# Moving the value transposes of the attention stage into the block of transposes behind Q's projection

## The chip, the core and the metric

The kernel runs on one core of one Trainium2 chip. The metric is the device time of one execution in microseconds (us). The engines are TensorE (PE: matmuls, and PEld for its weight loads), VectorE (DVE), ScalarE (ACT), GpSimd (POOL) and SyncE (SP), which here only issues DMAs. Each engine runs its own instruction stream in order, and the streams meet at semaphores that are written out by hand.

## The reference, cut to what matters

```python
x = x + attn(cond(x, cond_128, ...), w_attn, w_proj, adapter_wte, gating)
x = x + ffn(cond2(x, ...), ...)

def attn(x, w_attn, w_proj, adapter_wte, gating):      # 32 sequences of 64 tokens, 1024 channels, 32 heads of 32
    q, k, v = split(einsum('btc,oc->bto', x, w_attn), 3)
    q, k = rope(q), rope(k)
    y = softmax(causal(q @ k.T / sqrt(32))) @ v         # per head
    y = y + gating * softmax(q @ ak.T / sqrt(1024)) @ av  # 10 adapter rows, ak and av from the same w_attn
    return einsum('btc,oc->bto', y, w_proj)
```

The change touches only the attention, ahead of `w_proj`. What comes before it (mixing of `x`) and behind it (output projection, convolution, routed low-rank feed-forward) is as it was.

## The kernel before, in words

The attention stage is a loop over 8 groups `g` of 4 heads (128 channels) and, within each, over 4 units `u` of 512 tokens: 32 units, `n = 4 g + u`. In unit `n` TensorE projects K, Q and V of the unit, 24 matmuls of 128x512 each (three for each of 8 channel chunks, `project_qkv`; operands are split into a high and a low part, `w_hi` and `w_lo` for the weights), into the PSUM banks `bK`, `bQ` and `bV`. The attention proper lags by one unit: in unit `n` it is done for unit `n - 1`. TensorE's order in a unit is:

1. `attend_scores(n-1)`, 32 small matmuls (64 in the trace, which shows the two passes of a float32 matmul apart), line 903;
2. `turn_values(n-1)`, four 128x128 transposes of `vT` into `bV`, line 969;
3. the projections of K and Q, line 957; in the first unit of a group also `project_adapter`, line 981;
4. `attend_transposes(n-1)`, four transposes of the adapter weights (line 912) and eight of the softmax's result `prob` (line 919);
5. the projection of V, line 957;
6. `attend_values(n-1)`, two matmuls for the adapter (line 931, which read `aT`) and 32 small ones (line 940, which read `pT` and the values `vs`), into `bY` and, since no bank is free, into `bK`.

So the next K projection also waits until ScalarE has copied the half of `y` that lies in `bK`.

ScalarE copies V's projection out of PSUM (`vT`, line 1291), copies the turned values into `vs` (four copies, line 1304), takes the exponentials (lines 1187 and 1189), copies the transposed weights (`aT`, line 1194, `pT`, line 1197), and copies `y` (`ysb`, line 1203). VectorE masks and normalises the scores and rotates K and Q.

In the last unit of a group (`refill`, units 3, 7, ... 27: seven of them) the weights of the next group are brought in: SP issues one DMA of 1536 KB into `w_st` (line 759), and ScalarE rounds K's, Q's and V's third to `w_hi` (`split_hi`, line 1182), each in its place in the stream of its unit: K's ahead of `attend_copies`, Q's behind it, V's behind `vT`. VectorE then forms `w_lo` (`split_lo`, line 1371). SP issues that DMA behind the store of the last prepared weights (`store_prep`), which it issues behind the store of `y`. After the loop, the last unit's attention is interleaved with the output projection (line 1036).

Of the kernel before, what the change touches and what calls it, by code (L numbers as in the profile page):

```python
# [28 lines left out]
ACT = mybir.ActivationFunctionType  # L29
# [3 lines left out]
P = 128  # L33
NB, NC, L = 32, 64, 1024
# [3 lines left out]
NG = L // P  # L38
UT = 512
NU = TOK // UT  # L40
# [3 lines left out]
NP = NB // 2  # L44
# [23 lines left out]
Q_, K_, V_ = 0, 1, 2  # L68
# [5 lines left out]
def wait(eng, sem, value):  # L74

    if not isinstance(value, int) or value > 0:
        eng.wait_ge(sem, value)
# [304 lines left out]
def program(nc, d, psum, z, zbase, y_dram, x1_dram, w_forms, ctx_dram, aggb_dram, weights, out):  # L382
# [8 lines left out]
    with ExitStack() as ctx:  # L391
        def sem(name):
            return ctx.enter_context(nc.semaphore(name))
# [37 lines left out]
        ident = both.take("ident", [P, P])  # L431
# [17 lines left out]
        vT = sb("vT", [P, UT])  # L449
        vs = sb("vs", [P, UP // 2, 2, GH * HD])  # L450
# [41 lines left out]
        bS, bY, bQ, bK, bV = bank[0:4], bank[4], bank[5], bank[6], bank[7]  # L492
# [16 lines left out]
        v_tr = sem("a_v_tr")  # L509
        vs_set = sem("a_vs_set")  # L510
# [28 lines left out]
        y_mm = sem("a_y_mm")  # L539
        y_copied = sem("a_y_copied")  # L540
# [50 lines left out]
        def place(t):  # L591

            return t.manual_sbuf_range[0]

        parts, ctx_out, z_mm, z_sum, z_lo = mixing(
            nc, ctx, d, psum, z, z[:, :, :, :, :].bitcast(F32),
            [Space(nc, "f", zbase + u * Z + Z // 2).take(f"z_raw{u}", [P, KC, UT]) for u in range(NU)], ctx_dram, aggb_dram,
            (wst, whi, wlo, whi_f, w_first, w_hi, w_lo),
            (place(kbd_pad), place(qr), place(bbase), [place(t) for t in (x8[0], prob[0], pT[0], vs)],
             [place(t) for t in (vT, aprob, aT, ysb)], attn.at))  # L600
# [4 lines left out]
        def first(g, u):  # L605
            return isinstance(g, int) and g == 0 and u == 0

        def last(g):
            return isinstance(g, int) and g == NG - 1

        def refill(g, u):

            return u == NU - 1 and not last(g)

        def y_banks(m):

            return (bY, bK) if m < NG * NU - 1 else (bS[3], bS[0])

        def y_done(m):

            return 2 * (m + 1)

        def prep_at(n):

            g, u = n // NU, n % NU
            return 2 * g + u - 1 if u in (1, 2) else None
# [261 lines left out]
        def _(pe):  # L888
# [20 lines left out]
            def attend_transposes(m):  # L909
                pe.wait_ge(aprobs, 2 * m + 2)  # L910
                for i in range(UP):
                    tr = pe.transpose(bAT[:, i * P:(i + 1) * P], aprob[:, i, :].bitcast(F32),  # L912
                                      ident[:])
                tr.then_inc(a_tr, 1)
                wait(pe, pT_copied, 2 * m)
                for t, dst in enumerate(bPT):
                    pe.wait_ge(probs, 2 * m + t + 1)
                    for j in range(4):
                        tr = pe.transpose(dst[:, j * P:(j + 1) * P],  # L919
                                          prob[t][:, 2 * j:2 * j + 2, :].rearrange("p h k -> p (h k)"), ident[:])  # L920
                    tr.then_inc(p_tr, 1)
# [40 lines left out]
            def project_qkv(x, dst, g, u):  # L962
                for c in range(KC):
                    project_chunk(x, dst, g, u, c)

            def turn_values(m):
                pe.wait_ge(vT_copied, m + 1)
                for i in range(UP):
                    tr = pe.transpose(bV[:, i * P:(i + 1) * P], vT[:, i * P:(i + 1) * P], ident[:])  # L969
                tr.then_inc(v_tr, 1)  # L970

            def project_adapter(g, n):
# [13 lines left out]
            def unit_step(g, u):  # L986
                n = NU * g + u
                groups = g + 1 if u else g
                att = not first(g, u)
                if g == 0:  # L990
                    pe.wait_ge(z_lo, UP * (u + 1))
                if att:
                    attend_scores(n - 1, groups)
                    turn_values(n - 1)
                wait(pe, turned[K_], n)
                wait(pe, y_copied, y_done(n - 2) - 1)
                project_qkv(K_, bK, g, u)
                wait(pe, turned[Q_], n)
                project_qkv(Q_, bQ, g, u)
                if u == 0:  # L1000
                    project_adapter(g, n)
                if att:
                    attend_transposes(n - 1)
                wait(pe, vs_set, n)
                project_qkv(V_, bV, g, u)
                if att:
                    attend_values(n - 1, groups)
# [103 lines left out]
            m = NG * NU - 1  # L1111
# [53 lines left out]
        def _(act):  # L1165
# [10 lines left out]
            def split_hi(x, g, n):  # L1176

                act.wait_ge(w_in, 16 * g)
                wait(act, mm_done[x], n)
                if x != Q_:  # L1180
                    wait(act, akv_mm, g)
                act.activation(whi[:, :, x, :], wst[:, :, x, :], ACT.Copy).then_inc(w_hi[x], 1)
# [8 lines left out]
            def attend_copies(m):  # L1191
                act.wait_ge(a_tr, m + 1)
                wait(act, y_mm, m)
                act.activation(aT[:], bAT[:], ACT.Copy).then_inc(aT_copied, 1)  # L1194
                for t, src in enumerate(bPT):
                    act.wait_ge(p_tr, 2 * m + t + 1)
                    act.activation(pT[t][:].rearrange("p s q -> p (s q)"), src[:], ACT.Copy).then_inc(pT_copied, 1)

            def y_copy(m):
                act.wait_ge(y_mm, m + 1)  # L1200
                wait(act, y_out, 16 * m)
                for r in (1, 0):
                    act.activation(ysb[:].rearrange("p (s r t) -> p r s t", r=2, t=P)[:, r],
                                   y_banks(m)[r][:, 0:UP * NC].rearrange("p (s t) -> p s t", t=P), ACT.Copy).then_inc(y_copied, 1)
# [52 lines left out]
            def unit_step(g, u):  # L1257
                n = NU * g + u
                att = not first(g, u)
                if att:  # L1260
                    attend_exp(n - 1)
                if refill(g, u):
                    split_hi(K_, g + 1, n + 1)
                if n == 0:
                    for i in range(NP - 5, NP - 2):
                        mix_scalar.high(act, i)
                if u == 0:
                    act.wait_ge(akv_mm, g + 1)
                    wait(act, ak_tr, g)
                    act.activation(akv[:], bAD[:, 0:2 * P], ACT.Copy).then_inc(akv_copied, 1)  # L1270
                if n == 0:
                    mix_scalar.high(act, NP - 2)
                if att:
                    attend_copies(n - 1)
                if refill(g, u):
                    split_hi(Q_, g + 1, n + 1)
                if u == 0:
                    act.wait_ge(ak_tr, g + 1)
                    wait(act, scores, 2 * n)
                    act.activation(kbd[:, :, NC:KW], bAD[:, AKT:AKT + NA].rearrange("p (b a) -> p b a", b=1)  # L1280
                                   .broadcast_to([P, UB, NA]), ACT.Copy).then_inc(akbd_set, 1)
                if n == 0:
                    mix_scalar.high(act, NP - 1)
                if prep_at(n) is not None:
                    prep_high(prep_at(n))
                if n == NG * NU - 1:
                    for f in form_order(0)[:4]:
                        high(0, f)
                act.wait_ge(mm_done[V_], n + 1)
                wait(act, v_tr, n)  # L1290
                act.activation(vT[:], bV[:], ACT.Copy).then_inc(vT_copied, 1)
                if refill(g, u):
                    split_hi(V_, g + 1, n + 1)
                if n == NG * NU - 1:
                    high(0, S2)
                if att:
                    y_copy(n - 1)
                act.wait_ge(v_tr, n + 1)
                wait(act, y_mm, n)
                if n == 0:  # L1300
                    act.wait_ge(z_mm, NP)
                for b in range(2):
                    for r in range(2):
                        cp = act.activation(vs[NC * r:NC * (r + 1), :, b, :],  # L1304
                                            bV[NC * b:NC * (b + 1), :].rearrange("p (s r c) -> p r s c", r=2, c=P)[:, r],
                                            ACT.Copy)
                cp.then_inc(vs_set, 1)

            for n in range(NG * NU):
                unit_step(n // NU, n % NU)  # L1310
            m = NG * NU - 1
# [550 lines left out]
```

## Time and profile before

| | |
|---|---|
| median of 3 runs | 1137.48 us (1137.21 to 1139.59) |
| the profiled execution: time, span | 1138.46 us, 1136.7 us |
| PE busy | 1126.2 us, 99% of the span |
| DVE busy | 922.0 us, 81% |
| ACT busy | 361.1 us, 32% |
| chain that ended last | PE 86%, DMA 6%, DVE 3%, issue 3%, ACT 1%, SPq 1% |
| ACT L1304, `a_vs` | 128 copies, 48.5 us, 379 ns each |
| ACT L1182, `w_hi`, idle before it | 70.8 us, 7 times, until the DMA of `w_st` |

The span runs from the first to the last instruction; the time of an execution holds some 1.8 us around it. Matmuls overlap in the records, so the length of a block of them is read from start to start and not from the busy column. The mean granted clock of TensorE is 1.000 of full speed over the span.

### The profile page before, as it was taken

What the parts mean: (1) busy time and instruction counts of PE and PEld (TensorE: products, weight loads), DVE (VectorE), ACT (ScalarE), POOL (GpSimd) and SP (SyncE); (2) the same over time, 40 slices, a digit from 0 to 9 for tenths busy, and PEclk for the clock granted to TensorE, in tenths of its full rate; (3) what the DMA queues carried; (4) which work ended last, traced back from release to release, by engine and by line L of the source; (5) the groups of instructions that cost most, each with busy time, mean ns of one, the idle gap of its engine ahead of it and who ended that gap; (6) DMA issues with size and microseconds to landing.
All of it is one profiled execution on the core that took longest, in us unless ns stands there. A gap on an engine that the chain in (4) does not pass through costs nothing.

```text
span 1136.7 us, 23651 instructions
## 1 busy us (share of the span) xinstructions
PE 1126.2 (99%) x9688; PEld 947.3 (83%) x9688; DVE 922.0 (81%) x1740; ACT 361.1 (32%) x697; POOL 53.7 (5%) x23
## 2 busy tenths in 40 slices
PE   9999999999999999999999999999999999999998
PEld 6888788888888788888888888878888888888887
DVE  5999879879889789799798799888767777887674
ACT  5433333333342342433434334323222221222210
POOL 0000000000000000000000000110000022221112
PEclk9999999999999999999999999999999999999999
DMA  6515215114124025034133177884549933333312
GB/s 220 185 57 162 72 29 168 66 56 149 58 77 151 35 84 168 12 111 140 33 100 131 55 275 264 325 248 156 185 130 354 340 92 99 98 116 117 98 37 93
DMA packets 99708, 151.94 MB, mean 134 GB/s; under 512 B 7442, under 2 KB 84114, under 8 KB 96914
## 3 DMA queue, kind: packets, MB, share of 16 engines
q1 hardware_dynamic: 98594, 135.76, 36.8%
q10 hardware_dynamic: 1008, 14.68, 3.1%
q8 instruction: 77, 1.26, 0.5%
q14 instruction: 29, 0.24, 0.1%
HBM read 95.88 MB, written 54.54 MB: 132 GB/s over the span
## 4 chain that ended last, share of the span: by engine, by line
PE 86%; DMA 6%; DVE 3%; issue 3%; ACT 1%; SPq 1%; POOLq 0%; POOL 0%; DVEq 0%; ACTq 0%
PE psum L957 40%; PE psum L1036 23%; PE psum L1054 5%; PE psum L903 2%; PE psum L940 2%; PE psum L919 2%; PE psum L276 2%; DMA w_forms<-a_prep_hi_two 2%; DMA w_st<-in_wqkvT 2%; PE psum L1088 2%; DMA y_scratch<-a_ysb 2%; PE psum L1070 2%; PE psum L969 1%; PE psum L912 1%; PE psum L981 1%
## 5 line engine op out<-in xcount | busy, mean ns | idle before, releaser
L957 PE MATMUL psum<-z,w_hi 128*128 128x512 f32 x1536 | 481.9, 395 | 0.8 <-issue 0.6
L957 PEld LDWEIGHTS psum<-z,w_hi 128*128 128x128 f32 x1536 | 282.5, 188 | 57.9 <-issue 2.0
L957 PE MATMUL psum<-z,w_lo 128*128 128x512 f32 x768 | 300.3, 391 | 0.0
L1036 PE MATMUL psum<-f_wform,f_act_hi 128*128 128x512 f32 (+1 forms) x912 | 279.9, 389 | 2.0 <-DVE f_u L1506 1.4
L1036 PEld LDWEIGHTS psum<-f_wform,f_act_hi 128*128 128x128 f32 x912 | 167.9, 188 | 36.4 <-issue 2.8
L1036 PE MATMUL psum<-f_wform,f_act_lo 128*128 128x512 f32 (+1 forms) x456 | 176.1, 386 | 0.0
L957 PEld LDWEIGHTS psum<-z,w_lo 128*128 128x128 f32 x768 | 144.1, 188 | 31.5
L1036 PEld LDWEIGHTS psum<-f_wform,f_act_lo 128*128 128x128 f32 x456 | 85.7, 188 | 17.6
L878 POOL TENSOR_TENSOR f_xn<-f_x,_bbase 128x1024 f32<-128x1024 f32 x16 | 51.2, 3197 | 1033.2 <-DVE f_x L1532 701.6
L1231 ACT ACTIVATE f_act_hi<-f_act_sum 128x512 fp32r<-128x512 f32 x64 | 40.3, 632 | 119.5 <-DVE f_act_sum L1481 47.9
L1231 ACT ACTIVATE f_act_hi<-f_raw 128x512 fp32r<-128x512 f32 x56 | 33.7, 626 | 102.2 <-DVE f_raw L1564 64.5
L1406 DVE TENSOR_TENSOR a_prob<-psum,a_mask 128x512 f32<-128x512 f32 x64 | 44.0, 687 | 24.6 <-PE psum L903 24.6
L1487 DVE TENSOR_TENSOR f_act_lo<-f_act_sum,f_act_hi 128x512 fp32r<-128x512 f32 x64 | 49.0, 769 | 16.8 <-ACT f_act_hi L1231 16.8
L1487 DVE TENSOR_TENSOR f_act_lo<-f_raw,f_act_hi 128x512 fp32r<-128x512 f32 x56 | 37.2, 689 | 28.0 <-ACT f_act_hi L1231 27.9
L1194 ACT ACTIVATE a_aT<-psum 128x512 fp32r<-128x512 f32 x32 | 19.1, 598 | 122.0 <-PE psum L912 121.9
L1187 ACT ACTIVATE a_prob<-a_prob 128x512 f32<-128x512 f32 x64 | 40.5, 633 | 53.9 <-DVE a_prob L1411 53.3
L1304 ACT ACTIVATE a_vs<-psum 64x256 f32<-64x256 f32 x128 | 48.5, 379 | 25.2 <-PE psum L969 24.1
L1384 DVE STREAM_SHUFFLE a_rot<-psum 128x512 f32<-128x512 f32 x64 | 47.1, 736 | 0.0
L1411 DVE TENSOR_TENSOR a_prob<-a_prob,a_stat 128x512 f32<-128x512 f32 x64 | 44.3, 692 | 2.2
L1387 DVE TENSOR_TENSOR a_rot<-a_rot,a_sin 128x512 f32<-128x512 f32 x64 | 44.3, 692 | 2.2
L1423 DVE TENSOR_TENSOR a_prob<-a_prob,a_stat 128x512 f32<-128x512 f32 x64 | 44.3, 692 | 2.2
L1409 DVE TENSOR_REDUCE a_stat<-a_prob 128x8 f32<-128x512 f32 x64 | 43.9, 686 | 2.2
(172 smaller groups left out, 1478.2 us busy)
## 6 DMA issues: line engine op xcount, KB each, us to landing
w_forms<-f_prep_lo SPq DMA_DIRECT2D x16, 896.0 KB, 5.2
f_wform<-w_forms SPq DMA_DIRECT2D x7, 2048.0 KB, 13.6
f_wform<-w_forms ACTq DMA_DIRECT2D x7, 2048.0 KB, 17.6
w_st<-in_wqkvT SPq DMA_DIRECT2D x7, 1536.0 KB, 6.6
w_forms<-f_prep_hi SPq DMA_DIRECT2D x16, 640.0 KB, 6.2
m_x<-in_x SPq DMA_DIRECT2D x16, 512.0 KB, 5.4
y_scratch<-a_ysb SPq DMA_DIRECT2D x32, 256.0 KB, 2.8
f_raw<-y_scratch SPq DMA_DIRECT2D x8, 1024.0 KB, 5.8
```

The lines of the kernel that those rows point to most:

```text
L878: pool.tensor_tensor(xn[:, t, :].rearrange("p (m q) -> p q m", q=PH), x1[:, t, :].rearrange("p (q m) -> p q m", q=PH), bbase[:].rearrange( ...
L957: mm = pe.matmul(dst, w[:, c, x, :], zs, start=(c == 0 and i == 0), stop=(c == KC - 1 and i == 2))
L1036: mm = pe.matmul((prod_bank[i], bank[0])[part][:, cols], a[:, c, :], wform[i][:, w, c, cols], start=(i < 4 and c == 0 and n == 0), stop=(c ...
L1054: mm = pe.matmul(conv_banks(p)[:, o:o + P], x8[p % 2][:, CONV * b + g, j:j + P], toep[:, g, j, :], start=(j == 0), stop=(j == 1))
L1231: act.activation(act_hi[f][:], src, ACT.Copy).then_inc(act_hi_set, 1)
L1304: cp = act.activation(vs[NC * r:NC * (r + 1), :, b, :], bV[NC * b:NC * (b + 1), :].rearrange("p (s r c) -> p r s c", r=2, c=P)[:, r], ACT. ...
L1384: dve.stream_shuffle(rot[:], src[:], HALF_SWAP).then_inc(turned[x], 1)
L1387: dve.tensor_tensor(r, r, tab[1], ALU.mult).then_inc(rot_step, 1)
L1406: dve.tensor_tensor(prob[t][:].rearrange("p (h s) k -> p h s k", h=2), score_slots[:, 2 * t:2 * t + 2, :, 0:NC], maskb, ALU.add).then_inc( ...
L1411: dve.tensor_tensor(prob[t][:], prob[t][:], spread(t, 0), ALU.subtract).then_inc(shifted, 1)
L1423: dve.tensor_tensor(prob[t][:], prob[t][:], spread(t, 2), ALU.mult).then_inc(probs, 1)
L1487: dve.tensor_tensor(act_lo[f][:], src, act_hi[f][:].bitcast(F32), ALU.subtract).then_inc(act_set, 1)
```

## The change

`turn_values(n-1)` is moved from behind the scores to the head of the block of transposes behind Q's projection. Its result goes to the bank `bY` (`v_bank`), which is free there once `y` of unit `n - 2` is copied; only the last unit's transposes stay behind their scores and on `bV`. V's projection no longer waits for `vs`. On ScalarE the four copies into `vs` become `spread_values`, and stand ahead of `attend_copies` of the next unit, where they were behind `y_copy`. In the refill units `y_copy` now stands ahead of V's `split_hi`.

```diff
+        def v_bank(m):
+            return bY if m < NG * NU - 1 else bV
...
             def turn_values(m):
                 pe.wait_ge(vT_copied, m + 1)
+                if m < NG * NU - 1:
+                    wait(pe, y_copied, y_done(m - 1))
                 for i in range(UP):
-                    tr = pe.transpose(bV[:, i * P:(i + 1) * P], vT[:, i * P:(i + 1) * P], ident[:])
+                    tr = pe.transpose(v_bank(m)[:, i * P:(i + 1) * P], vT[:, i * P:(i + 1) * P], ident[:])
                 tr.then_inc(v_tr, 1)
...
                 if att:
                     attend_scores(n - 1, groups)
-                    turn_values(n - 1)
                 wait(pe, turned[K_], n)
...
                 if att:
+                    turn_values(n - 1)
                     attend_transposes(n - 1)
-                wait(pe, vs_set, n)
                 project_qkv(V_, bV, g, u)
...
+            def spread_values(m):
+                act.wait_ge(v_tr, m + 1)
+                wait(act, y_mm, m)
+                if m == 0:
+                    act.wait_ge(z_mm, NP)
+                for b in range(2):
+                    for r in range(2):
+                        cp = act.activation(vs[NC * r:NC * (r + 1), :, b, :],
+                                            v_bank(m)[NC * b:NC * (b + 1), :].rearrange("p (s r c) -> p r s c", r=2, c=P)[:, r],
+                                            ACT.Copy)
+                cp.then_inc(vs_set, 1)
...
                 if att:
+                    spread_values(n - 1)
                     attend_copies(n - 1)
...
                 act.activation(vT[:], bV[:], ACT.Copy).then_inc(vT_copied, 1)
-                if refill(g, u):
-                    split_hi(V_, g + 1, n + 1)
                 if n == NG * NU - 1:
                     high(0, S2)
                 if att:
                     y_copy(n - 1)
-                act.wait_ge(v_tr, n + 1)
-                wait(act, y_mm, n)
-                if n == 0:
-                    act.wait_ge(z_mm, NP)
-                for b in range(2):
...
+                if refill(g, u):
+                    split_hi(V_, g + 1, n + 1)
+                if n == NG * NU - 1:
+                    spread_values(n)
```

TensorE at the border of two units (units 1 and 2). Before, the last small matmuls of `attend_values`, the scores, V's transposes (`a_vT`), then K's projection:

```order
L940 MATMUL psum<-a_pT_111,a_vs 32x64 x2
L903 MATMUL psum<-a_kbd,a_qr 64x74 x32
L969 MATMUL psum<-_ident,a_vT 128x128 x4
L957 MATMUL psum<-z,w_hi 128x512 x2
L957 MATMUL psum<-z,w_lo 128x512
```

Of the change, at the same place (line numbers are those of the changed file):

```order
L944 MATMUL psum<-a_pT_111,a_vs 32x64 x2
L907 MATMUL psum<-a_kbd,a_qr 64x74 x32
L961 MATMUL psum<-z,w_hi 128x512 x2
L961 MATMUL psum<-z,w_lo 128x512
L961 MATMUL psum<-z,w_hi 128x512 x2
```

The projection now follows the scores with nothing between them.

TensorE behind Q's projection in unit 2. Before:

```order
L957 MATMUL psum<-z,w_lo 128x512
L912 MATMUL psum<-_ident,a_aprob 128x128 x4
L919 MATMUL psum<-_ident,a_prob_108 128x128 x4
L919 MATMUL psum<-_ident,a_prob_109 128x128 x4
L957 MATMUL psum<-z,w_hi 128x512 x2
L957 MATMUL psum<-z,w_lo 128x512
```

Of the change:

```order
L961 MATMUL psum<-z,w_lo 128x512
L975 MATMUL psum<-_ident,a_vT 128x128 x4
L916 MATMUL psum<-_ident,a_aprob 128x128 x4
L923 MATMUL psum<-_ident,a_prob_108 128x128 x4
L923 MATMUL psum<-_ident,a_prob_109 128x128 x4
L961 MATMUL psum<-z,w_hi 128x512 x2
L961 MATMUL psum<-z,w_lo 128x512
```

The block has grown from twelve transposes to sixteen.

ScalarE in the first refill unit, unit 3. Before, from the exponentials of unit 2 to the copies of the turned values of unit 3:

```order
L1187 ACTIVATE a_prob_109<-a_prob_109 128x512
L1189 ACTIVATE a_atmp<-a_atmp 128x160
L1182 ACTIVATE w_hi<-w_st 128x8x128
L1194 ACTIVATE a_aT<-psum 128x512
L1197 ACTIVATE a_pT_110<-psum 128x512
L1197 ACTIVATE a_pT_111<-psum 128x512
L1182 ACTIVATE w_hi<-w_st 128x8x128
L1291 ACTIVATE a_vT<-psum 128x512
L1182 ACTIVATE w_hi<-w_st 128x8x128
L1203 ACTIVATE a_ysb<-psum 128x2x128 x2
L1304 ACTIVATE a_vs<-psum 64x2x128 x4
```

Of the change:

```order
L1192 ACTIVATE a_prob_109<-a_prob_109 128x512
L1194 ACTIVATE a_atmp<-a_atmp 128x160
L1187 ACTIVATE w_hi<-w_st 128x8x128
L1211 ACTIVATE a_vs<-psum 64x2x128 x4
L1199 ACTIVATE a_aT<-psum 128x512
L1202 ACTIVATE a_pT_110<-psum 128x512
L1202 ACTIVATE a_pT_111<-psum 128x512
L1187 ACTIVATE w_hi<-w_st 128x8x128
L1309 ACTIVATE a_vT<-psum 128x512
L1220 ACTIVATE a_ysb<-psum 128x2x128 x2
L1187 ACTIVATE w_hi<-w_st 128x8x128
```

The four copies into `a_vs` (of unit 2) now stand between K's rounding and the copies of `aT` and `pT`, and the copies of `y` (`a_ysb`) have changed places with the last `w_hi`, V's.

## Rows read from the trace of the kernel before

**Rows 1.** The page, busy time of each engine.
```profile
PE 1126.2 (99%) x9688; PEld 947.3 (83%) x9688; DVE 922.0 (81%) x1740; ACT 361.1 (32%) x697; POOL 53.7 (5%) x23
```

**Rows 2.** Waits of PE: who for whom, us in total, times, longest.
```profile
PE psum L940 <- ACT a_pT L1197: 0.8, 3, 0.4
...
PE psum L969 <- ACT a_vT L1291: 0.4, 1, 0.4
```

**Rows 3.** Timeline of PE in an ordinary unit: start us, us, instruction.
```profile
160.85 0.60 PE L912 MATMUL psum<-_ident,a_aprob 128*128 128x128 f32 x4
161.28 1.04 PE L919 MATMUL psum<-_ident,a_prob 128*128 128x128 f32 x8
...
169.71 0.65 PE L969 MATMUL psum<-_ident,a_vT 128*128 128x128 f32 x4
170.12 0.72 PE L957 MATMUL psum<-z,w_hi 128*128 128x512 f32 x2
170.68 0.40 PE L957 MATMUL psum<-z,w_lo 128*128 128x512 f32 x1
170.91 0.40 PE L957 MATMUL psum<-z,w_hi 128*128 128x512 f32 x1
```

**Rows 4.** Timeline of PE where a wide product follows line 940 directly.
```profile
726.28 0.74 PE L1036 MATMUL psum<-f_wform,f_act_hi 128*128 128x512 f32 x2
726.87 0.40 PE L1036 MATMUL psum<-f_wform,f_act_lo 128*128 128x512 f32 x1
```

**Rows 5.** Timeline of ACT, the copies into `vs` in an ordinary unit.
```profile
170.40 1.55 ACT L1304 ACTIVATE a_vs<-psum 64x256 f32<-64x256 f32 x4 [0.88 <-PE psum L969]
```

**Rows 6.** Timeline of ACT in the first refill unit.
```profile
122.50 1.06 ACT L1182 ACTIVATE w_hi<-w_st 128x1024 fp32r<-128x1024 f32 x1 [11.03 <-DMA w_st<-in_wqkvT]
123.58 0.60 ACT L1194 ACTIVATE a_aT<-psum 128x512 fp32r<-128x512 f32 x1
124.08 1.08 ACT L1197 ACTIVATE a_pT<-psum 128x512 f32<-128x512 f32 x2
...
125.98 0.61 ACT L1291 ACTIVATE a_vT<-psum 128x512 f32<-128x512 f32 x1
126.45 1.08 ACT L1182 ACTIVATE w_hi<-w_st 128x1024 fp32r<-128x1024 f32 x1
127.40 0.68 ACT L1203 ACTIVATE a_ysb<-psum 128x256 f32<-128x256 f32 x2
```

**Rows 7.** Timeline of PE at the same place.
```profile
125.30 0.85 PE L940 MATMUL psum<-a_pT,a_vs 64*32 64x64 f32 x64 [0.44 <-ACT a_pT L1197]
126.17 0.93 PE L903 MATMUL psum<-a_kbd,a_qr 32*64 32x74 f32 x64
127.03 0.66 PE L969 MATMUL psum<-_ident,a_vT 128*128 128x128 f32 x4
127.91 0.70 PE L957 MATMUL psum<-z,w_hi 128*128 128x512 f32 x2 [0.22 <-issue]
```

**Rows 8.** Timelines of ACT and PE in the refill units of groups 1, 4 and 6.
```profile
205.16 1.06 ACT L1182 ACTIVATE w_hi<-w_st 128x1024 fp32r<-128x1024 f32 x1 [9.92 <-DMA w_st<-in_wqkvT]
...
210.73 0.49 PE L957 MATMUL psum<-z,w_hi 128*128 128x512 f32 x1
...
454.55 1.06 ACT L1182 ACTIVATE w_hi<-w_st 128x1024 fp32r<-128x1024 f32 x1 [9.27 <-DMA w_st<-in_wqkvT]
...
460.77 0.72 PE L957 MATMUL psum<-z,w_hi 128*128 128x512 f32 x2
...
620.64 1.06 ACT L1182 ACTIVATE w_hi<-w_st 128x1024 fp32r<-128x1024 f32 x1 [9.49 <-DMA w_st<-in_wqkvT]
...
627.09 0.70 PE L957 MATMUL psum<-z,w_hi 128*128 128x512 f32 x2 [0.21 <-issue]
```

**Rows 9.** Timelines of DVE and PE in unit 4: end of the softmax, first transposes.
```profile
138.30 0.23 DVE L1440 CAST a_aprob<-a_aprob 128x160 fp32r<-128x160 f32 x1
...
139.98 0.66 PE L912 MATMUL psum<-_ident,a_aprob 128*128 128x128 f32 x4
```

More of the change, by code:

```diff
@@ L1297, in unit_step @@
                     y_copy(n - 1)
-                act.wait_ge(v_tr, n + 1)
-                wait(act, y_mm, n)
-                if n == 0:
-                    act.wait_ge(z_mm, NP)
-                for b in range(2):
[L1303 to L1307, printed above, removed]
+                if refill(g, u):
+                    split_hi(V_, g + 1, n + 1)
+                if n == NG * NU - 1:
+                    spread_values(n)
             for n in range(NG * NU):
```

## The prediction

> **What bounds the kernel now.** I read the page first: TensorE is busy for 1126.2 of the 1136.7 us of the span [rows 1], so a change pays only where TensorE starts something sooner, or costs where it starts something later. Then the waits of TensorE: in the attention stage hardly any are left. The largest that belongs to the part changed is that of the small matmuls of `attend_values` for `pT`, 0.8 us over three places, and one wait of 0.4 us of the first value transposes for `vT` [rows 2]. So the change can't win much by taking waits away. What it can do is to alter the length of TensorE's own blocks, and to bring back waits where ScalarE is nearly late. Where that is, the timeline of ScalarE shows: in a refill unit it stands still for 11.03 us until the weights of the next group have landed, and all it has to do in that unit comes after, in a row [rows 6], while TensorE is some 2 us from needing it [rows 7]. I call the start of K's rounding L below (122.50 in the first such unit), and L is when the DMA has landed.
>
> **The 24 ordinary borders of units.** Removed: the four value transposes behind the scores, 169.71 to 170.12, so 0.41 us. Added: four in the block behind Q's projection. The four adapter transposes there last from 160.85 to 161.28, 0.43 us for the same shape, and I price the four new ones so [rows 3]. What a full-size float32 transpose costs where it stands between its like is thus known to 0.01 us; nothing is saved by their standing together. What isn't in the trace is a projection straight behind the small score matmuls. Nearest is the output product behind line 940: its first two matmuls take 726.28 to 726.87, 0.59 us [rows 4], against 0.56 us behind the transposes, 170.12 to 170.68 [rows 3]. So +0.03 us. A border costs 0.43 - 0.41 + 0.03 = +0.05 us, and 24 of them +1.2 us. The bounds: the two matmuls could follow at their steady pace (0.46 us, twice the 0.23 us from 170.68 to 170.91), which makes the border -0.08 us and the sum -1.9 us; at 0.1 us worse than line 940's case it is +3.6 us. I take the near row.
>
> That the small matmuls and the full ones don't mix freely is what the row of 0.59 us shows [rows 4]. The Trainium skill says under TensorEngine Tiling (Array Packing), Key Properties, that a change of tiling mode drains TensorE. By that rule the change removes no drain, since scores are followed by something full-size before and after; row and rule give the same +0.03 us here.
>
> At the first border the transposes now wait for `vT` for 0.4 us [rows 2]. Moved 11 us back they don't, and the scores' successor needs nothing of it: -0.4 us.
>
> **The wait for `vs` ahead of V's projection** goes. It is worth nothing: the copies end at 170.40 + 1.55 = 171.95 [rows 5], and V's projection of that unit starts some ten microseconds later. The Trainium skill, Perfetto Trace Analysis, Matmuls, advises rotating independent groups through PSUM banks so that an evacuation overlaps the next matmuls. The bank `bY` does that; by the rows the overlap was already complete, and the rule speaks for a gain that isn't there.
>
> **The seven refill units.** Here the order on ScalarE decides. Before: K's rounding at L, `aT` at L + 1.08, both `pT` until 125.16 = L + 2.66, then Q's rounding, `vT` at L + 3.48, V's rounding at L + 3.95, `y` at L + 4.90 [rows 6]. TensorE starts line 940 at 125.30, 0.14 us after `pT`, the scores 0.87 later, the transposes 0.86 after those, and the next K projection at 127.91 = L + 5.41, half a microsecond after `y` was begun [rows 7]. So the projection waits for the copy of `y`, which waits behind V's rounding.
>
> With the change the four copies into `vs` stand between K's rounding and `aT`. They take 1.55 us [rows 5], and everything behind them moves by 1.57. Their transposes are done before L, but ScalarE can't take them: it is held by the weights' DMA. So `pT` is done at L + 4.23, line 940 starts at L + 4.37, the scores at L + 5.24, and end at L + 6.10. The copy of `y` no longer stands behind V's rounding: `vT` at L + 5.05, `y` at L + 5.52, and the projection could start 0.51 later, at L + 6.03. The scores end later, so K's projection starts at L + 6.10. What the new order of `y` saves is used up by the delay of `pT`.
>
> Before, that start was at L + 5.41 in group 0; groups 2 and 3 show the same pattern, so three times. It was 210.73 - 205.16 = L + 5.57 in group 1, 460.77 - 454.55 = L + 6.22 in group 4, and 627.09 - 620.64 = L + 6.45 in group 6 [rows 8]; for group 5 I take 5.9, the mean of groups 1 and 4. Sum after less sum before: 7 x 6.10 - (3 x 5.41 + 5.57 + 6.22 + 5.9 + 6.45) = 42.7 - 40.4 = +2.3 us. This already leaves out the value transposes at the border, but not the four that come later in the unit: 7 x 0.43 = +3.0 us. The first two matmuls add 7 x 0.03 = +0.2. The refill units together: +5.5 us.
>
> L itself I leave where it is against TensorE: SP issues the weights' DMA behind the store of `y` of the unit before, which isn't moved, and the DMA itself isn't touched. `prep_high` on ScalarE moves back by the 1.55 us of the copies [rows 5] in units 1 and 2 of a group; VectorE takes its result only behind the rotation of Q, which is the work that hides it, so the stores ahead of the weights' DMA stay. If that cover is gone, each microsecond is one in L, at seven places.
>
> **What else moves.** In the unit behind a refill VectorE starts the softmax only after V's `w_lo`. V's rounding goes from L + 3.95 to behind `y`, L + 5.52 + 0.53 = L + 6.05: VectorE is 2.1 us later. Before, the last cast of `aprob` ended at 138.53, and its transposes began at 139.98, 1.45 us of slack [rows 9]. TensorE is itself 0.7 + 0.43 us later there, so 0.5 us is left: free, but only just. The last unit keeps its order, and nothing is put down for it.
>
> **Sum.** 5.5 + 1.2 - 0.4 = +6.3 us. Against the profiled execution's 1138.46 us that is 1144.8; that execution is 1.0 us above the median of the runs, so against the median, 1137.48, it is **1143.8 us**, 0.55% slower. What a measurement of this kernel can tell from no change is about 0.2%, 2.3 us.
>
> **Rivals.** (A) The delay of `pT` isn't on the path, because the weights land earlier against V's projection than I take it. From 1.6 us earlier on in group 0 (less in the others) only the borders count: 31 x 0.05 = +1.6, less 0.4, less the waits that fall away, 0.8 us [rows 2] and the half microsecond at the borders of groups 0, 2 and 3, 1.4 us. That is -1.0 us, 1136.5: not slower. For it speaks that L differs by group: K's projection starts 5.4 to 6.5 us behind it [rows 6 to 8]. Against it, nothing in the change starts the DMA earlier. 0.11.
> (B) As A, and the projection follows the scores at the steady pace: 31 x -0.08 = -2.5 in place of +1.6 for the borders, -5.1 us in all, 1132.4, faster. Against it stands the row of 0.59 [rows 4]. 0.04.
> (C) The 0.5 us of slack of the softmax isn't there, or `prep_high`'s cover is gone, and each of seven groups loses 0.5 to 1 us more: 1147.3 to 1150.8, slower still. For it speaks the thin slack [rows 9]. 0.10.
> My forecast has the remaining 0.75, with a range of its own of 1141 to 1146.5: the borders' bounds (-3.1, +2.4 us about their term), and 0.2 us at each refill.
>
> **Range and chances.** 1139.8 to 1147.5 leaves out A's and B's centres, and most of C. Slower by over 0.2%: forecast and C, 0.84, with 0.01 off for the forecast's lower end. Within 0.2%: most of A, 0.12. Faster: B, 0.04.
>
> **What the next profile would show.** Right: in the refill units the `vs` copies stand between K's `w_hi` and `aT`; line 940's successor starts 4.4 us behind K's `w_hi` and waits for `pT` in all seven; K's projection 6.1 us behind it. The ordinary unit grows by 0.05 us, with four transposes of 0.43 us at the head of its block. V's projection waits nowhere. Wrong: no wait at the small matmuls of `attend_values` (A), a border shorter than before (B), or a wait of the transposes for `aprob` in the first unit of a group (C).

## The result and the profile after

The changed kernel takes 1145.12 us (median of 6 runs, 1143.37 to 1148.89) against 1137.35 us for the kernel before in the same runs: a ratio of 1.0075, 95% interval 1.0061 to 1.0090. It is slower, by 0.75% where 0.55% was forecast, and 1145.12 lies in the range of 1139.8 to 1147.5. A second series, on another occasion, gave 1.0058 (1.0036 to 1.0080), so the forecast lies just below the first interval and inside the second. By the medians the loss is 7.8 us in the first series and 5.8 us in the second, where 6.3 us was forecast.

The page of the profiled execution (1145.06 us), its span and the busy times, and under it the first rows of TensorE's waits (engine, line, for whom: us in total, times, longest):

```profile
span 1143.3 us, 23650 instructions
...
PE 1128.8 (99%) x9688; PEld 949.7 (83%) x9688; DVE 926.9 (81%) x1740; ACT 360.2 (32%) x697; POOL 53.1 (5%) x23
```

```profile
PE psum L944 <- ACT a_pT L1202: 3.2, 7, 0.6
PE psum L935 <- ACT a_aT L1199: 2.9, 4, 1.3
```

The span has grown by 6.6 us, TensorE's busy time by 2.6. The wait of the small matmuls of `attend_values` for `pT` was 0.8 us at three places [rows 2] and is now 3.2 at seven, and a wait for `aT` has come, 2.9 us at four. Seven is the number of refill units. The wait of 0.4 us for `vT` is gone.

ScalarE in the first refill unit, the place of [rows 6]:

```profile
122.15 1.06 ACT L1187 ACTIVATE w_hi<-w_st 128x1024 fp32r<-128x1024 f32 x1 [10.42 <-DMA w_st<-in_wqkvT]
123.11 1.54 ACT L1211 ACTIVATE a_vs<-psum 64x256 f32<-64x256 f32 x4
124.67 0.60 ACT L1199 ACTIVATE a_aT<-psum 128x512 fp32r<-128x512 f32 x1
125.17 1.08 ACT L1202 ACTIVATE a_pT<-psum 128x512 f32<-128x512 f32 x2
126.12 1.07 ACT L1187 ACTIVATE w_hi<-w_st 128x1024 fp32r<-128x1024 f32 x1
127.07 0.61 ACT L1309 ACTIVATE a_vT<-psum 128x512 f32<-128x512 f32 x1
127.55 0.68 ACT L1220 ACTIVATE a_ysb<-psum 128x256 f32<-128x256 f32 x2
128.07 1.10 ACT L1187 ACTIVATE w_hi<-w_st 128x1024 fp32r<-128x1024 f32 x1
```

TensorE at the same place, beside [rows 7]:

```profile
125.32 0.50 PE L935 MATMUL psum<-a_aT,a_avbd 128*128 128x256 f32 x2 [0.43 <-ACT a_aT L1199]
126.39 0.85 PE L944 MATMUL psum<-a_pT,a_vs 64*32 64x64 f32 x64 [0.57 <-ACT a_pT L1202]
127.30 0.93 PE L907 MATMUL psum<-a_kbd,a_qr 32*64 32x74 f32 x64
128.16 0.73 PE L961 MATMUL psum<-z,w_hi 128*128 128x512 f32 x2
128.74 0.39 PE L961 MATMUL psum<-z,w_lo 128*128 128x512 f32 x1
```

With L = 122.15, the copies into `vs` start at L + 0.96, `pT` is done at L + 4.10, line 944 starts at L + 4.24, and K's projection at L + 6.01. ScalarE waited 10.42 us for the weights in all. For the last 4 us of this the turned values lay ready in PSUM (the four transposes end at 118.13), but their copies stand behind K's rounding in ScalarE's stream and had to wait with it.

An ordinary unit, beside [rows 3]: the value transposes now lead the block, and the projection follows the scores.

```profile
161.13 0.60 PE L975 MATMUL psum<-_ident,a_vT 128*128 128x128 f32 x4
161.57 0.60 PE L916 MATMUL psum<-_ident,a_aprob 128*128 128x128 f32 x4
...
162.80 0.71 PE L961 MATMUL psum<-z,w_hi 128*128 128x512 f32 x2
...
169.54 0.93 PE L907 MATMUL psum<-a_kbd,a_qr 32*64 32x74 f32 x64
170.40 0.73 PE L961 MATMUL psum<-z,w_hi 128*128 128x512 f32 x2
170.97 0.39 PE L961 MATMUL psum<-z,w_lo 128*128 128x512 f32 x1
```

In group 1 something more happened. Windows of the same execution (stretch: length, busy time and count by engine, granted clock, DMA): the wait at the end of unit 7, the first 3.3 us of K's projection of unit 8, and the 3 us after.

```profile
208.90:212.30 3.40, 1.56 (x68) 1.01 (x66) 0.65 (x1) 3.35 (x8) 0.00 (x0) 1.00 0.00 0
213.36:216.70 3.34, 3.34 (x12) 2.68 (x10) 2.55 (x4) 0.89 (x1) 0.00 (x0) 0.55 0.29 81
217.00:220.00 3.00, 3.00 (x15) 2.47 (x14) 2.90 (x6) 1.00 (x2) 0.00 (x0) 1.00 0.00 0
```

TensorE was busy for 1.56 of 3.40 us; then its clock was granted at about half, which is the 1.2 GHz level, and came back to full within 4 us. 9 matmuls start in those 3.34 us, where 13 start in the 3.00 us later (the counts in the rows take in those already running), and that unit is about 1.4 us longer than its like in the other groups (23.36 against 21.95 to 22.09 in five of them, from the start of one K projection to that of the next; group 6's 22.58 holds a gap that is told of at the end).

### The profile page after: what moved, and what is told of

It reads as the page before. It is cut to its first block, busy times and chain, and to the rows that moved or that the text cites. A ratio compares the mean times of both kernels' runs of the same rounds, so it can differ in the third digit from the quotient of the medians.

```text
span 1143.3 us, 23650 instructions
## 1 busy us (share of the span) xinstructions
PE 1128.8 (99%) x9688; PEld 949.7 (83%) x9688; DVE 926.9 (81%) x1740; ACT 360.2 (32%) x697; POOL 53.1 (5%) x23
## 4 chain that ended last, share of the span: by engine, by line
PE 79%; DMA 9%; DVE 4%; issue 3%; ACT 2%; SPq 2%; DVEq 0%; ACTq 0%
PE psum L961 35%; PE psum L1041 23%; PE psum L1059 5%; DMA w_st<-in_wqkvT 4%; DMA w_forms<-a_prep_hi_two 4%; PE psum L944 2%; PE psum L907 2%; PE psum L1093 2%; PE psum L1075 2%; PE psum L923 2%; DMA y_scratch<-a_ysb 2%; PE psum L276 1%; SPq L705 1%; PE psum L975 1%; PE psum L916 1%
## 5 line engine op out<-in xcount | busy, mean ns | idle before, releaser
L1381 DVE TENSOR_TENSOR w_lo<-w_st,w_hi 128x1024 fp32r<-128x1024 f32 x21 | 25.7, 1225 | 31.5 <-ACT w_hi L1187 31.5
```

## The experiments

All times and ratios are against the kernel before on the same chip. Its median was 1136.64 us in the series of the first four runs, 1138.98 in that of the next four and 1137.81 in that of the last two, so runs of different series are compared by their ratios, whose intervals are some 0.1% to either side. L is the start of K's rounding in a refill unit, as in the prediction.

**The copies into `vs` ahead of K's rounding.** Only the disputed 1.57 us are taken from behind the landing; `aT` and `pT` stay there.

```diff
                 if refill(g, u):
+                    spread_values(n - 1)
                     split_hi(K_, g + 1, n + 1)
...
                 if att:
-                    spread_values(n - 1)
+                    if not refill(g, u):
+                        spread_values(n - 1)
                     attend_copies(n - 1)
```

> The changed kernel with one thing moved: in the seven refill units the four copies into vs stand ahead of K's rounding (ahead of the wait for the weights' DMA) in place of behind it; aT and pT stay behind it. Theory 1 (the cost is the 1.57 us that the copies put between the landing and pT, seven times): pT ready 2.7 us behind the start of K's rounding again, line 944 starts 2.8 to 4.0 behind it in place of 4.25 in all seven, K's projection 4.5 to 5.7 in place of 6.0; 7 us and the dip of the clock in group 1 gone, about 1137 us. Rival 2 (the weights' DMA lands later against TensorE in the changed kernel, from its issue on): the landing stays 0.5 us late on average, most of the loss stays with it, 1142 or more. Rival 3 (the sixteen transposes in a block and the border without transposes cost more than priced, some 0.2 us in each of 31 units): 1144 or more.

Measured: 1135.71 us (11 runs) against 1136.64, ratio 0.9993 (0.9984 to 1.0003). The whole loss is gone. ScalarE and TensorE in the first refill unit:

```profile
117.93 1.55 ACT L1211 ACTIVATE a_vs<-psum 64x256 f32<-64x256 f32 x4 [6.43 <-PE psum L975]
122.00 1.06 ACT L1187 ACTIVATE w_hi<-w_st 128x1024 fp32r<-128x1024 f32 x1 [2.53 <-DMA w_st<-in_wqkvT]
123.09 0.60 ACT L1199 ACTIVATE a_aT<-psum 128x512 fp32r<-128x512 f32 x1
```

```profile
124.82 0.86 PE L944 MATMUL psum<-a_pT,a_vs 64*32 64x64 f32 x64
125.70 0.93 PE L907 MATMUL psum<-a_kbd,a_qr 32*64 32x74 f32 x64
126.56 0.73 PE L961 MATMUL psum<-z,w_hi 128*128 128x512 f32 x2
```

Line 944 starts at L + 2.82 and K's projection at L + 4.56 (over the groups 2.81 to 4.13 and 4.53 to 5.91); the same 1.55 us of copies now lie in the wait for the DMA. The landing did not move: 15.72 us behind the start of K's projection here in group 0, 15.64 in the changed kernel. Rivals 2 and 3 fall, but for one place. In group 1 the weights again landed late and TensorE waited 0.5 us for `pT`: there rival 2 is right, for half a microsecond.

**All the copies ahead of K's rounding.** Nothing of the attention waits for the weights any more.

```diff
-                if refill(g, u):
-                    split_hi(K_, g + 1, n + 1)
...
                 if att:
                     spread_values(n - 1)
                     attend_copies(n - 1)
                 if refill(g, u):
+                    split_hi(K_, g + 1, n + 1)
                     split_hi(Q_, g + 1, n + 1)
```

> The changed kernel with K's rounding moved behind both the copies into vs and those of aT and pT in the refill units, so that nothing of the attention waits for the weights' DMA. Theory 1: line 944 waits for pT nowhere, the refill units are as long as ordinary ones (20.3 us), about 1136 us. Rival 2: the weights' landing then matters only if K's rounding and its w_lo come too late, which they don't by 3 us, so also about 1136; the pair with the run before tells how much late landing costs by itself. Rival 3: 1143 or more.

Measured: 1135.29 us (11 runs), ratio 0.9983 (0.9975 to 0.9992). No wait for `pT` or `aT` is left:

```profile
119.45 0.60 ACT L1199 ACTIVATE a_aT<-psum 128x512 fp32r<-128x512 f32 x1
119.95 1.08 ACT L1202 ACTIVATE a_pT<-psum 128x512 f32<-128x512 f32 x2
122.22 2.01 ACT L1187 ACTIVATE w_hi<-w_st 128x1024 fp32r<-128x1024 f32 x2 [1.19 <-DMA w_st<-in_wqkvT]
```

The refill units take 20.28 to 20.36 us, as ordinary ones.

**The kernel before, with its copies ahead of K's rounding.** The same edit on the old kernel (there are no `spread_values`): was the order already costing something?

```diff
-                if refill(g, u):
-                    split_hi(K_, g + 1, n + 1)
...
                 if att:
                     attend_copies(n - 1)
                 if refill(g, u):
+                    split_hi(K_, g + 1, n + 1)
                     split_hi(Q_, g + 1, n + 1)
```

> The kernel before with only K's rounding moved behind the copies of aT and pT in the refill units; V's transposes as before. Theory 1 (ScalarE's order behind the landing is what costs, before the change too): the refill units fall from 20.3 to 21.25 to 20.3 us, 2.8 us in all, about 1134.5 us. Rival (those units are long for another reason, such as the stores of the prepared weights on the DMA engines): 1137.

Measured: 1135.12 us (12 runs), ratio 0.9995 (0.9984 to 1.0005). By the time this is no difference that can be told. By the trace the mechanism is as forecast: the seven refill units take 20.31 to 20.34 us, and from the first K projection behind the scores to the output projection 641.4 us pass against 644.2 before, 2.8 us less. The profiled execution lost its gain ahead of that, in a wait of 1.91 us for a part of `x`, which the edit doesn't touch, and in a fall of TensorE's clock right behind it: its first scores start 2.9 us later than in the kernel before. It is one of three such: nine of the 12 runs took 1134.72 to 1135.50 us, the other three 1137.76 to 1140.54. The median is 1.5 us below that of the kernel before, but the ratio, which takes in all the runs, does not reach the expected 0.25%. So the trace bears the theory out and the timed ratio does not show it.

**Moved in ordinary units only.** In the refill units the transposes stand behind the scores on V's bank again, with the copies behind `y`.

```diff
+        def moved(n):
+            return n < NG * NU and not refill(n // NU, n % NU)
...
         def v_bank(m):
-            return bY if m < NG * NU - 1 else bV
+            return bY if moved(m + 1) else bV
...
                 if att:
-                    turn_values(n - 1)
+                    if moved(n):
+                        turn_values(n - 1)
                     attend_transposes(n - 1)
+                if not moved(n):
+                    wait(pe, vs_set, n)
```

(and, where a unit is not moved, the transposes behind the scores, and on ScalarE `spread_values` behind `y_copy` and V's rounding)

> V's transposes moved in the 24 ordinary units only; the seven refill units have them behind the scores on V's bank, with the copies into vs behind y as before, and y ahead of V's rounding. Theory 1: no refill cost, first border 0.8 us shorter, last unit 0.4 longer, y ahead of V's rounding saves 0.5 us at three or four borders; 1135 to 1136 us. Rival 3: 24 x 0.2 us = 5 us of the loss stays, 1141 or more.

Measured: 1135.09 us (11 runs), ratio 0.9988 (0.9979 to 0.9997). Nothing of the loss is in the ordinary borders: it stands in the seven refill units.

**`y` behind V's rounding.** The change's second half is undone.

```diff
+                if refill(g, u):
+                    split_hi(V_, g + 1, n + 1)
                 if att:
                     y_copy(n - 1)
-                if refill(g, u):
-                    split_hi(V_, g + 1, n + 1)
```

> The changed kernel with y_copy behind V's rounding again in the refill units (as before the change), all else as changed. Theory 1: vT is copied 4.9 us behind the start of K's rounding, V's rounding 5.4, y 6.35, so K's projection of the next unit starts 6.9 behind it in place of 6.0, waiting for y; seven times 0.85 us, 6 us slower than the change, 1151. Rival: the copy of y is hidden behind the scores and its place is worth nothing, 1145.

Measured: 1148.66 us (4 runs), ratio 1.0078 (1.0055 to 1.0101). K's projection starts at L + 6.85 in all seven, as expected:

```profile
124.19 1.06 ACT L1187 ACTIVATE w_hi<-w_st 128x1024 fp32r<-128x1024 f32 x1 [8.98 <-DMA w_st<-in_wqkvT]
...
130.54 0.68 ACT L1220 ACTIVATE a_ysb<-psum 128x256 f32<-128x256 f32 x2
```

```profile
131.04 0.70 PE L961 MATMUL psum<-z,w_hi 128*128 128x512 f32 x2 [0.65 <-issue]
```

So the place is worth 0.85 us at each refill unit, if the delay of `pT` is there. The expected 1151 us, 6 us above the changed kernel, was not seen in the total: this ratio can't be told apart from the changed kernel's 1.0075 or 1.0058. In the two traces the refill units are 5.5 us longer together, and the units behind them 2.5 us shorter. Of these, 1.4 are the fall of the clock, which this execution didn't have, and 0.6 the gap in group 6's; the last half microsecond is spread over the groups, perhaps because the weights of the first matmul had long been loaded, which no run shows. (In group 0 the weights landed 1.4 us earlier against TensorE, and `pT` wasn't waited for; the wait for `y` came all the same.)

**The copies doubled.** Four more copies of the same shape, from the same bank into an unused buffer, in the refill units.

```diff
+                if m + 1 < NG * NU and refill((m + 1) // NU, (m + 1) % NU):
+                    for b in range(2):
+                        for r in range(2):
+                            act.activation(spare[NC * r:NC * (r + 1), 2 * P * b:2 * P * (b + 1)].rearrange("p (s c) -> p s c", c=P),
+                                           v_bank(m)[NC * b:NC * (b + 1), :].rearrange("p (s r c) -> p r s c", r=2, c=P)[:, r],
+                                           ACT.Copy)
```

> The changed kernel with the four copies of the values doubled in the refill units (the extra four go to an unused buffer, behind K's rounding too). Theory 1: line 944 starts 5.8 us behind K's rounding in place of 4.25, K's projection 7.6 in place of 6.0, 7 x 1.55 = 11 us slower than the change, 1156; and where the wait of TensorE is longer than the 2.5 us that went ahead of the fall of its clock in the changed kernel's group 1, another 1.5 us each, up to 1165. Rivals 2 and 3 (late landing, or the borders): below 1150.

Measured: 1160.65 us (4 runs), ratio 1.0177 (1.0150 to 1.0204). Line 944 starts at L + 5.80 or 5.81 in all seven, as expected, and K's projection at L + 7.53 to 7.69 in groups 3 to 6 (7.6 was expected), but at L + 8.22 in groups 0 to 2. The waits:

```profile
PE psum L935 <- ACT a_aT L1199: 12.8, 7, 2.4
PE psum L944 <- ACT a_pT L1202: 4.0, 7, 0.6
```

The two waits have grown from 6.1 to 16.8 us together, 10.7 more, where 7 x 1.55 = 10.9 was expected. In groups 0 to 2 the clock fell as well, which is what makes their K projection late. The first:

```profile
126.00:130.40 4.40, 2.82 (x130) 2.42 (x130) 1.23 (x1) 4.38 (x9) 0.00 (x0) 0.69 0.02 4
130.50:134.00 3.50, 3.50 (x12) 2.80 (x9) 3.00 (x4) 0.40 (x1) 0.00 (x0) 0.50 0.27 75
134.20:138.00 3.80, 3.80 (x18) 3.10 (x17) 3.63 (x9) 1.56 (x3) 0.00 (x0) 0.96 0.00 0
```

**The kernel before with `y` ahead of V's rounding**, nothing else.

```diff
-                if refill(g, u):
-                    split_hi(V_, g + 1, n + 1)
                 if n == NG * NU - 1:
                     high(0, S2)
                 if att:
                     y_copy(n - 1)
+                if refill(g, u):
+                    split_hi(V_, g + 1, n + 1)
```

> The kernel before with y_copy ahead of V's rounding in the refill units, nothing else. Theory 1: the border behind a refill unit no longer waits for y in groups 0, 2 and 3, 0.47 us each: 1.4 us faster than the kernel before, 0.12%. Whether the similar gap of group 6 (0.45 us, where the copy of y was done long before) goes too tells whether it is the same wait. Rival: another wait of the same length stands behind it, and the time is that of before.

Measured: 1136.61 us (12 runs) against 1138.98, ratio 0.9973 (0.9960 to 0.9985). In group 0, where [rows 7] had a gap, the projection now follows the transposes at their pace:

```profile
129.39 0.66 PE L969 MATMUL psum<-_ident,a_vT 128*128 128x128 f32 x4
129.80 0.71 PE L957 MATMUL psum<-z,w_hi 128*128 128x512 f32 x2
```

K's projection is at L + 4.94 in groups 0, 2 and 3, 0.47 us earlier than L + 5.41. In group 6 it is at L + 6.60, so the gap there stays: it is not the wait for `y`. The refill units are 1.9 us shorter together in the trace, where 1.4 was expected. The timed gain, 0.15 to 0.40% or 1.7 to 4.6 us, is larger than expected and holds the trace's figure only at its lower end. Half of the change alone is a gain, of about 0.15% at the least.

**Moved in units 1 to 30, all copies ahead of K's rounding.** As the second experiment, with the last unit left as it was; written on the code of the fourth.

```diff
         def moved(n):
-            return n < NG * NU and not refill(n // NU, n % NU)
+            return n < NG * NU - 1
...
-                if refill(g, u):
-                    split_hi(K_, g + 1, n + 1)
...
                 if refill(g, u):
+                    split_hi(K_, g + 1, n + 1)
                     split_hi(Q_, g + 1, n + 1)
```

> V's transposes moved in units 1 to 30 but not in the last, and K's rounding behind all the copies in refill units. Theory 1: the first border keeps its 0.8 us, the last unit doesn't pay 0.4, refill units are as long as ordinary ones: 3.5 to 4 us faster than the kernel before, 0.3%. Rival: within 0.1% of before.

Measured: 1135.75 us (12 runs) against 1138.98, ratio 0.9976 (0.9963 to 0.9988): 3.2 us by the medians, where 3.5 to 4 were expected. The rival, within 0.1%, falls.

**The changed kernel again**, unedited.

> The changed kernel once more, for a second trace and a ratio on the chip of the run below. Theory 1: K's projection 6.0 us behind K's rounding in all seven refill units, whatever the landing; where TensorE waits 2.5 us or more for aT and pT together, its clock falls behind it, where it waits 1.5 us or less it doesn't always. Rival 2: the landing of group 1's weights 8.2 us after issue was chance and the refill units cost 1.5 us less this time; then the group's dip is gone too.

Measured: 1143.61 us (7 runs) against 1137.81, ratio 1.0058 (1.0036 to 1.0080). Waits:

```profile
PE psum L944 <- ACT a_pT L1202: 3.6, 7, 0.6
PE psum L935 <- ACT a_aT L1199: 2.7, 4, 1.0
```

K's projection starts at L + 5.97 to 6.13. The late landing of group 1 is there again, so it was not chance; the fall of the clock isn't. The longest waits for `aT` and `pT` together were 1.6 us here, so the part of the expectation on waits of 2.5 us or more was not put to a test by this run. The doubled copies speak against it: in their group 3 TensorE waited 1.94 and 0.57 us, 2.5 in all, and its clock stayed full.

**Moved in unit 1 only, copies ahead of K's rounding, `y` ahead of V's.**

```diff
         def moved(n):
-            return n < NG * NU - 1
+            return n == 1
```

> V's transposes moved in unit 1 only (where they wait for vT), K's rounding behind the copies of aT and pT, y ahead of V's rounding. Theory 1: 0.8 us at the first border less 0.4 in its block, 2.8 us in the refill units: 3.3 us faster than the kernel before, 0.3%, the same as with the transposes moved in units 1 to 30, since an ordinary border costs and gives nothing. Rival: moving them in all units is worth something of its own, and this is 1 us slower than that.

Measured: 1135.43 us (11 runs) against 1137.81, ratio 0.9973 (0.9962 to 0.9985), not to be told from the 0.9976 of the version with the transposes moved in 30 units. The two intervals could hide the rival's 1 us; the traces don't: from the first scores to the output projection 642.7 us pass here and 643.1 there. Every refill unit takes 20.29 to 20.31 us. This version, the one with units 1 to 30 moved and the kernel before with `y` ahead are each 0.24 to 0.27% faster than the kernel before.

## Why the prediction was right, step by step

**The refill units** (forecast +5.5 us). This was the step that carried the forecast, and it held. Line 944 starts at L + 4.24 or 4.25 in all seven groups (forecast 4.37), K's projection at L + 5.97 to 6.13 (forecast 6.10). Taking the copies out from behind the landing takes the whole loss away, doubling them adds 10.7 of 10.9 us, and moving the transposes everywhere but in these units costs nothing. The seven refill units are 5.0 us longer than before. What the order of `y` saves, I said, the delay of `pT` uses up: each half was then run alone. `y` alone is a gain of 0.27% (0.15 to 0.40), and without it the changed kernel starts K's projection 0.85 us later still. By the forecast's own terms: from L to K's projection the seven units take 1.8 us more than before (forecast 2.3), and up to L they take 3.2 us more (forecast 3.2, the four transposes and the first two matmuls).

**The landing stays where it is against TensorE** (forecast 0). Right on balance: counted from the end of the scores, the landings of six groups moved by -0.6 to +0.2 us, together -1.0. In group 1 it was wrong, +1.3 us (16.41 against 15.07): the weights landed 8.24 us after issue, where it was 6.62 in the kernel before, and this is no chance of one execution. Issue on SP and K's rounding on ScalarE in the changed kernel, then in the version with units 1 to 30 moved:

```profile
198.99 0.35 SPq L763 DMA_DIRECT2D w_st<-in_wqkvT  x1
```

```profile
207.23 1.06 ACT L1187 ACTIVATE w_hi<-w_st 128x1024 fp32r<-128x1024 f32 x1 [11.26 <-DMA w_st<-in_wqkvT]
```

```profile
197.22 0.35 SPq L767 DMA_DIRECT2D w_st<-in_wqkvT  x1
```

```profile
204.13 2.02 ACT L1196 ACTIVATE w_hi<-w_st 128x1024 fp32r<-128x1024 f32 x2
```

It took 8.0 to 8.4 us in all six traces of kernels that have the transposes moved in every unit (the changed kernel twice among them), and 6.3 to 6.9 in the six others. Among these is the version with units 1 to 30 moved, which up to that point runs the same instructions as the second experiment's kernel. (In that version and the second experiment's, K's rounding stands behind the copies, so 6.9 is an upper bound; the landing itself was 6.76 us after issue.)

The packets in the traces show what came between. Queues in the stretch from 5.5 to 8.0 us behind the issue (kind: packets, MB, share of 16 engines), in the changed kernel:

```profile
q1 hardware_dynamic: 11, 0.04, 4.8%
q8 instruction: 1, 0.02, 2.4%
```

and in the version with units 1 to 30 moved:

```profile
q1 hardware_dynamic: 12, 0.05, 4.8%
```

The one packet of queue 8, which the profile calls "instruction", holds 16 KB and takes 0.95 us. In all six late landings it starts 5.7 to 6.2 us behind the issue, and in five of them the last of the weights' 128 packets starts as it ends and takes 0.94 us in place of 0.46. In the six others such a packet came between 0.6 us ahead of the issue and 0.3 us behind it. That is a coincidence in twelve of twelve traces, not an experiment: no run moved that packet, why it comes later in some kernels is open, and in group 0, where one starts 4.8 to 5.4 us behind the issue in every trace, the weights landed after 6.2 to 7.5 us. A late landing costs TensorE as much as L moves where `pT` hangs on it: 1.3 us in the changed kernel's trace, 1.1 in its second.

**The clock.** Not in the forecast. One fall in group 1 cost 1.4 us of the profiled execution's 6.6. The second trace has none.

**The ordinary borders** (forecast +1.2 us, -1.9 to +3.6). The sign was wrong, the size small. The new transposes take 161.13 to 161.57, 0.44 us, as priced. The first two matmuls behind the scores take 0.57 us (170.40 to 170.97), against 0.56 before and 0.59 forecast. But the projections of K and Q together take 11.02 us, against 11.04, and V's behind the block 5.54 against 5.57, which no step had. An ordinary unit mostly takes 20.29 us where it took 20.31: -0.02, for all of them together -0.1. The rule of the Trainium skill, TensorEngine Tiling (Array Packing), Key Properties, that a change of tiling mode drains TensorE, is in keeping: from the start of the last score matmul to that of the next full-size one it is 0.153 us (median of 32) in both kernels, whatever follows. No run here shows the drain itself, and the page has no figure for it; the forecast's 0.03 us came from the row alone.

**The first border** (forecast -0.4 us). Right: scores to projection take 0.86 us where scores, wait and transposes took 1.70, and 0.41 of these 0.84 us comes back at the end of the loop, where from the last K projection ahead of the output projection to that one it is 20.80 us against 20.39.

**The wait for `vs` ahead of V's projection** (forecast 0). Right: with it gone, most ordinary units are 0.02 us shorter and none more than 0.07. The Trainium skill's advice on rotating banks (Perfetto Trace Analysis, Matmuls) had nothing to win here.

**The slack of the softmax** (forecast 0.5 us left). Right. In unit 4 the last cast of `aprob` starts at 139.93 and ends at 140.17; its transposes start at 140.76, 0.59 us later (0.55 to 0.69 in five groups, more in groups 1 and 6):

```profile
139.93 0.24 DVE L1450 CAST a_aprob<-a_aprob 128x160 fp32r<-128x160 f32 x1
...
140.76 0.49 PE L916 MATMUL psum<-_ident,a_aprob 128*128 128x128 f32 x3
```

**The sum.** From the first scores to the output projection the changed kernel's trace is 6.8 us longer, of 6.3 forecast: refill units +5.0, the units behind them +2.3 (the fall of the clock and a gap of half a microsecond in group 6 are 2.1 of it), ordinary ones -0.1, first border -0.4. The mechanism of the forecast was right and gives most of the loss. That the sum came within half a microsecond is partly luck: the forecast was 0.5 us too high in the refill units and 1.3 too high in the ordinary ones, and these misses were made up by 2.3 us that it had no term for. (The forecast's own range of 1141 to 1146.5 is also narrower than its terms make it: its borders' bounds alone reach down to 1140.7, and 0.2 us at each of seven refills adds 1.4 to either side.) Without the fall of the clock, as in the second trace, the same stretch is 5.4 us longer.

## What to carry to other kernels

An engine that is busy for a third of the span can still be what the kernel waits for, for two microseconds behind a DMA that it is made to await in order. So, when work is moved along such an engine, look for the instruction in its stream that waits for a transfer, and ask of each thing behind it whether it needs that transfer: 1.55 us of copies behind the landing cost 7 us in seven places, and ahead of it, nothing. And try the halves of a change apart: this one was a gain and a loss together.

## What the hardware showed that was not expected

- TensorE's granted clock fell to its lower level for some microseconds behind a stretch with waits, but the length of the wait alone doesn't tell where. It fell behind waits of 1.27 and 0.57 us in group 1 of the changed kernel, and didn't behind waits of 1.0 and 0.6 us there in the second trace. With `y` behind V's rounding the waits in group 1 were again 1.27 and 0.57 us, with 0.81 for `y` behind them, and the unit after took 21.90 us: no fall. With the copies doubled it fell in groups 0 to 2, where `aT` came 2.1 to 2.4 us late, and not in groups 3 to 6, where it came 1.2 to 1.9 us late. And it fell near the start of the kernel before with its copies ahead, behind a wait of 1.91 us for `x`.
- Two kernels that differ only from unit 30 on had a DMA of 1536 KB land 8.15 and 6.76 us after its issue in unit 7. In the first, a 16 KB packet of the instruction queue starts 6.16 us behind the issue, in the second 0.26 us behind it.
- The gap of half a microsecond (0.2 to 0.4 us of it idle in the rows) at the border behind group 6's refill unit stayed when `y` was copied early, and turned up in the changed kernel too, inside the projection. It waits for no semaphore that the profile shows. Its place in TensorE's stream is always the same, ahead of the fifth matmul behind the scores, and in the five traces that have it a 16 KB packet of the instruction queue ended 1.3 to 1.6 us before that matmul started; in the seven without it, 1.6 to 4.1 us before. So a wait for instructions would fit, but no run tested it.
